# Two-layer graph network on one core: a third spectra buffer, a negated filter half moved to ScalarE, and work moved forward around the second stage

## The reference

```
# layer 0
adj_hat = adj + I;  deg = sum(adj_hat, -1)
x = x + relu((D^-1/2 adj_hat D^-1/2 @ h) @ W.T + b)
# layer 1, with h from the new x, hc = h transposed
c  = relu(bn1(conv1d(hc, conv1_w)))            # 1 tap
c  = bn2(conv1d(c, conv2_w, pad=8))            # 17 taps along the nodes
x_conv = relu(c + hc)
s = h @ w_se.T + b_se;  A = exp(-dist(s, s))
x_nmp = A @ relu(h @ w_msg.T + b_msg)
gi = [x_conv, x_nmp] @ w_ih.T + b_ih;  gh = h @ w_hh.T + b_hh
r = sigmoid(gi_r + gh_r);  z = sigmoid(gi_z + gh_z)
n = tanh(gi_n + r * gh_n)
x = x + (1 - z) * n + z * h
```

## Time and profile before

| | |
|---|---|
| median of 3 runs | 1967.2 us (1966.85 to 1967.31) |
| profiled execution | 1968.26 us, span of the core 1966.4 us |
| TensorE busy | 1908.1 us, 97% of the span |
| VectorE, ScalarE, GpSimd busy | 59%, 51%, 43% |
| mean granted TensorE clock | 0.988 |
| TensorE's share of the chain that ended last | 91% |

### The profile page before, as it was taken

The page is one execution under the profiler, slowest core; times in us unless marked ns, Lnnn a source line. Parts: engine busy times, 40 slices in busy tenths (PEclk is TensorE's granted clock), DMA queues, the critical chain, the costliest instruction groups (busy, mean ns, idle before and its releaser), DMA issues.

```text
span 1966.4 us, 29930 instructions
## 1 busy us (share of the span) xinstructions
PE 1908.1 (97%) x10524; PEld 1673.6 (85%) x10524; DVE 1166.2 (59%) x2227; ACT 1010.5 (51%) x1794; POOL 838.6 (43%) x1054
## 2 busy tenths in 40 slices
PE   4999999999999998999989999999999999999998
PEld 4999999999999997888767888888888888888887
DVE  6889888999877746656663344443444343444433
ACT  3888888888888864444442332332333233323322
POOL 4778878888676624544541212221221122122211
PEclk7999999999999999999999999999999999999999
DMA  5445555555555344556653223223322332232221
GB/s 167 155 166 197 200 196 177 189 190 198 193 185 172 129 138 109 140 136 154 181 161 113 87 91 113 85 95 102 113 85 85 113 100 89 94 113 85 92 99 54
DMA packets 254994, 262.59 MB, mean 134 GB/s; under 512 B 96519, under 2 KB 204423, under 8 KB 252798
## 3 DMA queue, kind: packets, MB, share of 16 engines
q1 hardware_dynamic: 254846, 260.68, 42.1%
HBM read 151.57 MB, written 109.05 MB: 133 GB/s over the span
## 4 chain that ended last, share of the span: by engine, by line
PE 91%; DMA 2%; DVE 2%; issue 1%; ACT 1%; POOL 0%; SPq 0%; DVEq 0%; ACTq 0%; POOLq 0%
PE P L104 72%; PE P L604 5%; PE P L867 5%; PE P L654 3%; PE P L633 3%; DMA xl<-xh_d 2%; PE P L975 1%; PE P L625 1%; DVE wh0l L734 1%; ACT wh0h L727 0%; DVE wh0l L737 0%; DVE yo L774 0%; ACT xh0h L707 0%; DMA yt<-y_d 0%; SPq L691 0%
## 5 line engine op out<-in xcount | busy, mean ns | idle before, releaser
L851 POOL TENSOR_TENSOR xnx1l<-xnf,xnx1h 128x1024 fp32r<-128x1024 f32 x16 | 44.5, 2778 | 376.3 <-ACT xnx1h L844 376.3
L851 POOL TENSOR_TENSOR xnx0l<-xnf,xnx0h 128x1024 fp32r<-128x1024 f32 x15 | 41.8, 2784 | 340.5 <-ACT xnx0h L844 340.5
L948 DVE SCALAR_TENSOR_TENSOR gn<-tr,gn 128x512 f32<-128x512 f32 x64 | 44.3, 692 | 202.7 <-ACT tr L935 202.7
L935 ACT ACTIVATE tr<-P,cold 128x512 f32<-128x512 f32 x64 | 44.2, 690 | 217.2 <-PE P L104 217.2
L535 POOL TENSOR_TENSOR axl<-af,axh 128x512 fp32r<-128x512 f32 x64 | 83.5, 1305 | 137.3 <-ACT axh L361 137.3
L938 ACT ACTIVATE nn<-gn,col 128x512 f32<-128x512 f32 x64 | 46.3, 723 | 181.2 <-DVE gn L952 181.2
L959 DVE SCALAR_TENSOR_TENSOR tz<-tz,tr 128x512 f32<-128x512 f32 x64 | 44.3, 693 | 152.3 <-ACT tz L942 152.3
L942 ACT ACTIVATE tz<-P,cold 128x512 f32<-128x512 f32 x64 | 44.1, 689 | 166.5 <-PE P L104 166.5
L714 POOL TENSOR_TENSOR xh0l<-xl,xh0h 128x512 fp32r<-128x512 f32 x40 | 69.7, 1765 | 113.2 <-ACT xh0h L707 113.2
L604 PE MATMUL P<-ft,h 128*128 128x240 f32 x512 | 114.2, 366 | 1.2 <-DVE x L445 0.6
L867 PEld LDWEIGHTS P<-gt,yt 128*128 128x128 f32 x768 | 108.3, 191 | 5.7 <-DMA yt<-y_d 0.9
(11 more groups left out here) (193 smaller groups left out, 6783.3 us busy)
## 6 DMA issues: line engine op xcount, KB each, us to landing
xh_d<-xst SPq DMA_DIRECT2D x16, 1280.0 KB, 7.1
xl<-xh_d SPq DMA_DIRECT2D x40, 512.0 KB, 6.4
y_d<-yo SPq DMA_DIRECT2D x80, 256.0 KB, 2.3
x<-in_x SPq DMA_DIRECT2D x64, 256.0 KB, 2.9
a<-in_adj SPq DMA_DIRECT2D x64, 256.0 KB, 4.1
at<-in_adjt SPq DMA_DIRECT2D x64, 256.0 KB, 4.7
x_d<-x SPq DMA_DIRECT2D x64, 256.0 KB, 4.5
xn_d<-xt SPq DMA_DIRECT2D x64, 256.0 KB, 4.7
```

The lines of the kernel that those rows point to most:

```text
L851: e.e.tensor_tensor(o[1][:, :, :], xnf[p % 2][:, :, :, :].rearrange("p c i t -> p c (i t)"), o[0][:, :, :], ALU.subtract).then_inc(done, 1)
L948: e.e.scalar_tensor_tensor(out=gn[:, :], in0=tr[:, :], scalar=1.0, in1=gn[:, :], op0=ALU.add, op1=ALU.mult).then_inc(S["v"], 1)
```

## The change

Five things are changed, all in the second stage or at its ends.

1. The spectra have three buffers (`xh[f % 3]`). ScalarE copies, and GpSimd splits, bin f + 2 while bin f runs, behind the weights of bin f + 1 and no longer ahead of them. The room comes from `nmx[0]`, which moves out of the part of memory that lies behind the second stage's buffers; its split therefore comes after the last bin.
2. The high part's negation is done by ScalarE from `wf` (a new semaphore, `wnhi`), the low part's stays with VectorE.
3. Four filter units of the second part run before bin 0 (`AHEAD`), and ScalarE's copy of bin 0's spectra stands ahead of its last two unit copies.
4. The loads: spectra are loaded by SP at odd bins; the six gate weights one per bin from bin 30 to 35, `xn` at 36, `nm` at 38 and 39.
5. For n = 0 the gate products are put in another order, and TensorE waits for the output copies bank by bank.

The diff, cut to its core:

```diff
-        xh = [p2.hl(f"xh{i}", [128, 2, 2, 256]) for i in range(2)]
+        xh = [p2.hl(f"xh{i}", [128, 2, 2, 256]) for i in range(3)]
...
-        nmx = [early.hl("nmx0", [128, 2, 512])]
...
-        nmx.append(p3.hl("nmx1", [128, 2, 512]))
+        nmx = [p3.hl(f"nmx{i}", [128, 2, 512]) for i in range(2)]
...
+        AHEAD = 4
         def units_in(f, chunk):
             part, m = f // 10, 2 * (f % 10) + chunk
             if part == 3 or m >= 18:
                 return range(0)
-            return range(UNITS * (part + 1) + UNITS * m // 18, UNITS * (part + 1) + UNITS * (m + 1) // 18)
+            first = AHEAD if part == 0 else 0
+            n = UNITS - first
+            first += UNITS * (part + 1)
+            return range(first + n * m // 18, first + n * (m + 1) // 18)
...
         def spectra_hi(e, f):
             e.wait_ge(S[f"lxh{f // 2 % 2}"], 2 * loaded(f // 2, 2))
-            e.wait_ge(S["frq"], 2 * f - 2)
+            e.wait_ge(S["frq"], 2 * f - 4)
             for c in range(2):
-                t = e.e.copy(by_group(xh[f % 2][0], c), bin_of(f, c))
+                t = e.e.copy(by_group(xh[f % 3][0], c), bin_of(f, c))
...
             e.e.copy(both(wh[f % 2][0]), weights_of(f)).then_inc(S["whi"], 1)
+            e.e.mul(wh[f % 2][0][:, :, 0, :], weights_of(f)[:, 1, :, :], -1.0).then_inc(S["wnhi"], 1)
...
-            for t in (h, l):
-                d = e.e.tensor_scalar(t[:, :, 0, :], t[:, :, 2, :], -1.0, None, ALU.mult)
-            d.then_inc(S["wneg"], 1)
+            e.e.tensor_scalar(l[:, :, 0, :], l[:, :, 2, :], -1.0, None, ALU.mult).then_inc(S["wneg"], 1)
...
+            e.wait_ge(S["ye0"], NF - 1)
             e.wait_ge(S["gn"], n)
             gate(e, p, o, HN, 2, [4, 5], True, True).then_inc(S["ghn"], 1)
+            e.wait_ge(S["ye1"], NF - 1)
+            e.wait_ge(S["tr"], n)
+            gate(e, p, o, R, 0, [4, 5], True, False)
+            if n == 0:
+                e.wait_ge(S["ye1"], NF)
+                gate(e, p, o, Z, 1, [4, 5], True, False)
+                middle()
...
+            gate(e, p, o, R, 0, [2, 3], False, False)
+            if n == 0:
+                e.wait_ge(S["ye0"], NF)
+                gate(e, p, o, IN, 2, [2, 3], True, False)
+                gate(e, p, o, Z, 1, [2, 3], False, False)
...
             gate(e, p, o, R, 0, [0, 1], False, True).then_inc(S["gr"], 1)
+            if n == 0:
+                gate(e, p, o, IN, 2, [0, 1], False, True).then_inc(S["gin"], 1)
+                gate(e, p, o, Z, 1, [0, 1], False, True).then_inc(S["gz"], 1)
+                return
...
-                if f % 2 == 0 and f // 2 + 1 < NF // 2 and f:
-                    load_spectra(e, f // 2 + 1)
-                if f == 30:
-                    for c in range(6):
-                        load_wg(e, c)
+                if f % 2 and (f + 3) // 2 < NF // 2:
+                    load_spectra(e, (f + 3) // 2)
+                if 30 <= f < 36:
+                    load_wg(e, f - 30)
+                if f == 36:
                     load_pair(e, 0)
...
             for n in range(0, UNITS, 2):
+                if n == UNITS - 4:
+                    first_stage_done(e)
+                    spectra_hi(e, 0)
                 unit_out(e, n)
-            first_stage_done(e)
             weights_hi(e, 0)
-            spectra_hi(e, 0)
+            for n in range(UNITS, UNITS + AHEAD, 2):
+                unit_out(e, n)
+            spectra_hi(e, 1)
             for f in range(NF):
                 if f + 1 < NF:
-                    spectra_hi(e, f + 1)
                     weights_hi(e, f + 1)
+                if f + 2 < NF:
+                    spectra_hi(e, f + 2)
...
-            for n in range(UNITS):
+            for n in range(UNITS + AHEAD):
                 filter_unit(e, n)
```

More of the change, by code:

```diff
@@ L113 @@
 dist af am axhi axlo nmp nm snm dft0 dft1 xe0 xe1 sxh0 sxh1
-unit yz wev0 wev1 lxh0 lxh1 xhi xlo whi wlo wneg frq ye0 ye1 sy0 sy1 sy2 sy3
+unit yz wev0 wev1 lxh0 lxh1 xhi xlo whi wlo wneg wnhi frq ye0 ye1 sy0 sy1 sy2 sy3
 lwg0 lwg1 lwg2 lwg3 lwg4 lwg5 wghi wg ly0 ly1 ly2 lxn0 lxn1 lnm0 lnm1 nmhi nmlov nmlop xnhi xnlov xnlop
@@ L663, in unit_out @@
             e.wait_ge(S["unit"], n + 1)
-            e.wait_ge(S["whi"], 10 * (part - 1))
+            e.wait_ge(S["wnhi"], 10 * (part - 1))
             e.wait_ge(S["wlo"], 10 * (part - 1))
@@ L711, in spectra_lo @@
             e.wait_ge(S["xhi"], f + 1)
-            e.wait_ge(S["frq"], 2 * f - 2)
+            e.wait_ge(S["frq"], 2 * f - 4)
             for c in range(2):
-                t = e.e.tensor_tensor(by_group(xh[f % 2][1], c), bin_of(f, c), by_group(xh[f % 2][0], c), ALU.subtract)
+                t = e.e.tensor_tensor(by_group(xh[f % 3][1], c), bin_of(f, c), by_group(xh[f % 3][0], c), ALU.subtract)
             t.then_inc(S["xlo"], 1)
@@ L746, in freq @@
             e.wait_ge(S["wneg"], f + 1)
+            e.wait_ge(S["wnhi"], f + 1)
             e.wait_ge(S[f"ye{chunk}"], f - 1)
-            xb, wb = xh[f % 2], wh[f % 2]
+            xb, wb = xh[f % 3], wh[f % 2]
             def x_(h, c, q):
@@ L784, in load_wg @@
         def load_wg(e, c):
-            e.wait_ge(S["whi"], 30)
+            e.wait_ge(S["wnhi"], 30)
             e.wait_ge(S["wlo"], 30)
@@ L914, in gates_tensor @@
             e.wait_ge(S["nmlop"], 2 * p)
-            e.wait_ge(S["tr"], n)
-            gate(e, p, o, R, 0, [4, 5, 2, 3], True, False)
-            middle()
+            gate(e, p, o, R, 0, [2, 3], False, False)
[3 more added lines that the diff above has]
+                gate(e, p, o, Z, 1, [2, 3], False, False)
             e.wait_ge(S["xchi"], 2 * p + 2)
@@ L1026, in _ @@
             for f in range(NF):
-                if f % 2 == 0 and f // 2 + 1 < NF // 2 and f:
-                    load_spectra(e, f // 2 + 1)
-                if f == 30:
-                    for c in range(6):
-                        load_wg(e, c)
+                if f % 2 and (f + 3) // 2 < NF // 2:
[3 more added lines that the diff above has]
+                if f == 36:
                     load_pair(e, 0)
-                    for b in range(2):
-                        load_nm(e, b)
+                if f > 37:
+                    load_nm(e, f - 38)
                 for chunk in range(2):
@@ L1104, in _ @@
                     split_xn_hi(e, 0)
-                    for n in range(2):
-                        split_nm_hi(e, n)
             e.wait_ge(S["frq"], 2 * NF)
+            for n in range(2):
+                split_nm_hi(e, n)
             gates_scalar(e, 0, 0, lambda: (branch_scalar(e, 0), branch_scalar(e, 1)), lambda: None)
@@ L1167, in _ @@
             weights_lo(e, 0)
+            for n in range(UNITS + 1, UNITS + AHEAD, 2):
+                unit_out(e, n)
             for f in range(NF):
@@ L1181, in _ @@
                     split_xn_lo(e, 0, S["xnlov"])
-                    for n in range(2):
-                        split_nm_lo(e, n, S["nmlov"])
             e.wait_ge(S["frq"], 2 * NF)
+            for n in range(2):
+                split_nm_lo(e, n, S["nmlov"])
             branch_vector(e, 0)
```

1 line of the change is left out of this document (removed).

## The result

| | before | after |
|---|---|---|
| median on the device | 1967.0 us (1966.2 to 1967.3, 4 runs) | 1932.6 us (1930.9 to 1934.2, 4 runs) |
| profiled execution, span | 1968.26, 1966.4 us | 1933.19, 1931.4 us |
| mean granted clock | 0.988 | 0.994 |

The ratio of the medians is 0.9826 [0.9809, 0.9843]: the kernel is faster by 34.4 us.

What follows compares the result with a forecast made beforehand. The prediction took TensorE as the bound, with its waits and low-clock matmuls in the second stage to win. Terms of 31.2 us less 1.2 took 1968.3 to 1938.3, a median of 1937.2 us; range 1934 to 1946.

Steps and rivals of the forecast that it cites:

- The bound: Whole kernel: bound by TensorE; the second stage can give back its idle time and matmuls run at the lower clock.
- the start: Before bin 0: idle time falls from 5.86 to 0.64 us, gain 5.2, plus 2.1 of low clock won.
- the seven waits: Bins 10, 20, 30, 32, 34, 36, 38: TensorE's waits for VectorE's negation go, 14.8 us, plus 4.8 of low clock.
- the change doesn't do what it says: Rival: pauses at even bins stay because they come from SP's queue, not the chain; 1955 us, chance 0.04.
- Sum: Second stage and its ends: gains 5.2 + 2.1 − 0.6 + 14.8 + 4.8 + 4.9 = 31.2 us, less 1.2.
- The gates' start: End of bin 39 (T) to next inverse transform: gain 4.9 us, bounds 3 and 5.5; `yt` no earlier than T + 5.7.
- The allowance of 1.2 us: Set against the summed gain for small new waits that couldn't be placed, such as loads beside gate weights.
- The range: Median time: 1934 to 1941 us for the forecast case, 1934 to 1946 overall.
- Bin 1: Start of bin 1: a new wait of 0.6 us, bounds 0 and 1.5, as VectorE's difference meets GpSimd's split.
- DMA as the bound: Rival, bins 30 to 35: 264 GB/s needed where engines moved 214, so loads come late; 1944 us, chance 0.19.
- Slower: Rival: in-order ScalarE, held by the spectra load, delays outputs and next weights in 19 pairs; 1978 at 2.2 us each, chance 0.03.
- only the ends gain: Rival, bins: spectra still late as their load is issued no earlier; half of 14.8 and all 4.8 lost, 1948, chance 0.05.

## Why the prediction was right in its mechanism and wrong in its size

**The bound, the start and the seven waits: right.** Bin 0 started at 746.25 where I had 746.75 (the units also ended 0.5 us earlier), with 0.63 us of idle time for 0.64. All seven later waits and the low clock behind them went. Taking the buffer out brings the waits back, so the chain was the cause and not SP's queue by itself (where the block of gate weights stands in it, the queue lengthens the chain, as at bin 34); "the change doesn't do what it says" falls.

**"Sum", the first failed step: a pause was priced at its idle time.** Over the bins I had 26.3 us and the trace shows 28.2. Seven pauses account for 1.6 of the difference, 0.23 each. Two experiments give nearly the same price by other pauses: 0.29 with two buffers and 0.27 with VectorE's negation. The trace of before had it: bins 32 and 33 run from 983.54 to 1000.03 − 5.36 = 994.67, 11.13 us for 48 matmuls, 0.17 above four chunks of 2.74. The records show where it lies, here at bin 34 with two buffers:

```profile
982.95 0.39 PE L104 MATMUL P<-wh1h,xh1l 128*128 128x512 f32 x1
985.10 0.47 PE L104 MATMUL P<-wh0h,xh0h 128*128 128x512 f32 x1 [1.77 <-DVE wh0l L742]
985.41 0.39 PE L104 MATMUL P<-wh0l,xh0h 128*128 128x512 f32 x1
```

Without a pause such a matmul begins every 0.23 us though each record lasts 0.39. The idle time counts from the end of the last record, so 0.16 us are lost ahead of it, and the second matmul behind the pause begins 0.31 us after the first, 0.08 late: 0.24 in all. So it is behind each of the waits at the bins that full clock follows: the second begins 0.30 to 0.31 us after the first.

**"The gates' start", the second: `yt` at T + 5.7 was taken as a floor.** The transforms began at T + 4.2 (1016.96), as soon as the 18 products in front of them had ended, and nothing waited. The small part of the load takes from 2.5 to 4.7 us from its issue (last section), and the 5.7 was one value of it. My bounds of 3 to 5.5 don't hold the 6.1 that came, because they fixed a landing time that differs between the traces. Why it came early here is open. The other half of the step holds: the wait of 3.1 us and the lost clock hang on the order of the products, as the run with the old order shows.

**The allowance of 1.2 us** for waits that I couldn't place had no row under it and nothing came. With the sum of 31.2 as it stood, the forecast would have been 1936.0, still 3.4 us above what came.

**The range.** My best cases (0.7 at bin 0, 0.6 at bin 1, 0.6 at the gates, no allowance of 1.2) make 3.1 us, which reaches 1934.1, the low end that I gave. The price of a pause and the run-to-run spread of 2 us were in no bound, and `yt` only at its slow landing. The missing 4.6 us are 1.9 up to the end of the bins, 1.2 at the gates and 1.2 of allowance; 0.7 lies outside the stage, and 0.4 goes against it for rounding and the difference between profile and median.

**Bin 1** was forecast to wait 0.6 us. The price of the shared memory access was nearly right, 3.8 us from GpSimd's start to the end of all for 4.3: the negation took 1.40 us there and 0.43 alone, and VectorE's two instructions and GpSimd's split, from 746.66 on, were over only at 749.08 + 1.40 = 750.48. The start was wrong: the weight copy of bin 0 began 0.6 us earlier (743.13 for 743.76), and I added whole durations of ScalarE's instructions where each begins 0.1 us before the last is over (744.09 behind 743.13 + 1.05). So GpSimd began at 746.66 and not at 747.5, and all was ready 0.3 us before TensorE. The Trainium skill (SBUF — State Buffer, section "SBUF: two separate sides") has the port pair that the two share. By that rule one stands while the other's instruction runs; the trace agrees, as GpSimd's split took 3.54 us there and 2.50 at bin 0.

**DMA as the bound: falls, with little to spare.** Bins 31 to 36, two at a time:

```profile
963.80:974.70 10.90, 10.90 (x49) 9.03 (x49) 6.53 (x6) 7.14 (x11) 6.83 (x6) 1.00 1.03 272
974.70:985.60 10.90, 10.90 (x49) 9.01 (x49) 7.41 (x9) 7.89 (x13) 5.29 (x5) 1.00 1.00 264
985.60:996.50 10.90, 10.90 (x49) 9.01 (x48) 7.51 (x9) 7.90 (x13) 5.48 (x5) 1.00 1.03 271
```

My estimate of 264 GB/s was the rate within 3%, and the engines are full for 33 us, yet TensorE is busy for all 10.90 us of each. What shows the nearness is ScalarE, which waits 2.2 us for one load and 1.0 to 1.1 for three later ones. The longest:

```profile
962.15 1.14 ACT L712 CAST xh2h<-xl 128x512 fp32r<-128x512 f32 x2 [2.18 <-DMA xl<-xh_d]
```

0.26 MB more per bin, with the wait that it puts into SP's queue, already puts it in front of TensorE. The rival's price (214 GB/s) took the rate of one microsecond inside a spectra load as that of the mixture.

**What I priced at nothing.** The prediction gave the spread of the gate weights no term of its own. It came out in the right total, since the buffers' gain was counted with it, but alone it is worth 7.3 us, more than the negation. The negation had no term of its own either, and is worth 5.5 us in the bins. From my text nobody could have told which of the five parts may be left out.

**Slower, only the ends gain**: both fall. In bins 30 to 39 no weight copy began more than 0.1 us late behind a load, and both halves of a load had landed 6.9 to 7.9 us after its issue began.

## What to carry to other kernels

Price a pause of the bounding engine at its idle time plus the start-up around it (here 0.2 to 0.3 us), measured on the pauses of the trace itself. Where several steps of one chain are shortened, the waits go only when the last one is, so ask for each step what the chain looks like without it; here the spreading of the loads, which had no term in my sum, was worth 7 us. On an engine that works in order, a copy that waits for a load delays everything behind it, so the lead of that load against the next urgent instruction is the number to watch. It was about 1 us: a load that landed 2.6 us later cost TensorE 1.8, and one that landed 5.8 later (the block) cost 4.9.

## What the runs showed of the hardware

**A small load behind a large one lands at differing times.** The 64 KB part of `yt`, changed kernel first, then the one with VectorE's negation; same instructions, same order. Columns: start, us, engine, line, what.

```profile
1013.93 0.38 SPq L798 DMA_DIRECT2D yt<-y_d  x1
1014.35 0.51 SPq L800 DMA_DIRECT2D yt<-y_d  x1
...
1016.96 3.60 PE L872 MATMUL P<-gt,yt 128*128 128x128 f32 x24
```

```profile
1018.84 0.38 SPq L798 DMA_DIRECT2D yt<-y_d  x1
1019.27 0.51 SPq L800 DMA_DIRECT2D yt<-y_d  x1
...
1023.41 3.30 PE L872 MATMUL P<-gt,yt 128*128 128x128 f32 x24 [1.66 <-DMA yt<-y_d]
```

2.6 us from the issue in the one, 4.1 in the other; over the thirteen profiles with this order of the two parts it landed after 2.5 to 4.7. With the small part first the transforms began 3.6 us after the first issue (3.0 and 4.6 here), between the two, and that is a single execution. The landing took 3.9 or more in four of the five profiles with the old order of the gates and in one of the eight with the new. Whether that order has a part in it isn't shown, and the cause stays open.

**The kernel's first 50 us differ between executions.** The 26th unit's end lay between 740.4 and 743.7 us in the profiles, though nothing ahead of it was changed but the place of one copy; the part behind the gates' start was 902.7 to 903.3 us in all. The difference is there early: a matmul of the first stage (`w1m` with `xxh`) began between 46.2 and 49.4 us, and from it to the 26th unit all took 694.2 to 695.1 us. That is why the stage's own length was the better measure. The granted clock of those first 50 us differs too, from 0.76 to 0.90, but not in step: with 0.76 the unit ended at 741.6, with 0.90 at 741.6 and 742.8. So the clock isn't shown to be the cause.

**The length of a pause doesn't decide alone whether the low clock follows.** With ScalarE's negation alone there is a pause of 1.9 us up to 982.05 and one of 3.6 us up to 998.39. Behind the shorter the clock fell, behind the longer it didn't (columns as in the earlier trace rows):

```profile
984.00:986.00 2.00, 2.00 (x6) 1.54 (x5) 1.33 (x1) 0.00 (x0) 1.05 (x1) 0.50 1.04 397
...
998.00:1000.00 2.00, 1.61 (x7) 1.40 (x8) 2.00 (x4) 1.38 (x2) 2.00 (x2) 1.00 0.26 99
```

The earlier trace rows have the same: low behind 3.10 and 5.36, full behind 3.31. Over all traces from 740 to 1070 us, the shortest pause with low clock behind it was 1.90 us and the longest without it 3.56; none of the pauses up to 1.77 was followed by it. What else decides stays open.
